# One selective-scan stage: C rows by broadcast transfers, two decay slots, seven drives on GpSimd, the sum three places behind

## The reference, cut to what matters

```python
sel = jnp.einsum('ble,se->bls', xc, sel_w)
dt_in = sel[..., :R_]
Bm = sel[..., R_:R_ + N_]
Cm = sel[..., R_ + N_:]
dt = jax.nn.softplus(jnp.einsum('blr,er->ble', dt_in, dt_w) + dt_b)
dA = jnp.exp(dt[..., None] * A)
dBu = dt[..., None] * Bm[:, :, None, :] * xc[..., None]
def step(h, inp):
    dA_t, dBu_t, C_t = inp
    h = dA_t * h + dBu_t
    y = jnp.einsum('ben,bn->be', h, C_t)
    return (h, y)
```

## Time and profile before

| | |
|---|---|
| time, median of 3 runs | 1578.91 us (1573.58 to 1582.68) |
| the profiled execution: its own time | 1573.16 us |
| its span in the trace | 1571.4 us |
| scan stage of one pair, first drive to last output instruction | about 129.5 us, four times |
| mean granted TensorE clock | 0.959 |

### The profile page before, as it was taken

How to read it: one execution, slowest core, us unless ns; L and a number is a source line. 1 busy time by engine, 2 the same in 40 slices (tenths; PEclk the granted TensorE clock), 3 DMA queues, 4 the chain that set the end, 5 groups by cost and what they waited for, 6 DMA issues and landing times. The chain is left out here.

```text
span 1571.4 us, 16757 instructions
## 1 busy us (share of the span) xinstructions
PE 1370.2 (87%) x5750; PEld 564.0 (36%) x5770; DVE 1079.3 (69%) x1253; ACT 689.0 (44%) x979; POOL 415.8 (26%) x242
## 2 busy tenths in 40 slices
PE   6877899988987779999997778999999777899897
PEld 2222233346422223325632222332563222333265
DVE  3598956674559995667455998556746699765673
ACT  0455543334245554324425554532541655543344
POOL 3256610012006660002100766000300276500040
PEclk9989999998999999999898999999989899999997
DMA  8100020000000002000000000200000000020000
GB/s 255 72 0 1 1 57 11 1 1 1 14 0 0 1 1 67 2 1 1 1 14 0 0 1 0 68 1 1 1 1 14 0 0 1 4 51 1 0 2 14
DMA packets 24692, 26.02 MB, mean 17 GB/s; under 512 B 4610, under 2 KB 21794, under 8 KB 24098
## 3 DMA queue, kind: packets, MB, share of 16 engines
q1 hardware_dynamic: 24002, 20.61, 4.5%
q10 hardware_dynamic: 608, 4.34, 0.9%
HBM read 20.73 MB, written 4.21 MB: 16 GB/s over the span
## 5 line engine op out<-in xcount | busy, mean ns | idle before, releaser
L405 POOL TENSOR_TENSOR scratch<-scratch 128x1024 f32<-128x1024 f32 x124 | 306.1, 2468 | 467.3 <-ACT scratch L872 312.1
L1081 DVE TENSOR_TENSOR_SCAN scratch<-ps,scratch 128x1024 f32<-128x1024 f32 x128 | 292.2, 2283 | 5.5 <-ACT ps L865 5.5
L551 PE MATMUL ps<-scratch,consts 128*128 128x512 f32 x512 | 255.6, 622 | 14.0 <-ACT work L896 12.0
L416 POOL TENSOR_TENSOR work<-work,rmax 128x512 f32<-128x512 f32 x64 | 67.4, 1053 | 614.3 <-DVE rmax L1231 614.3
L865 ACT ACTIVATE ps<-steps,vec 128x1024 f32<-128x1024 f32 x128 | 143.1, 1118 | 183.4 <-DVE scratch L1081 183.4
L1133 DVE TENSOR_TENSOR scratch<-scratch,ps 128x1024 f32<-128x1024 f32 x108 | 131.9, 1221 | 117.8 <-PE ps L610 114.8
L905 ACT ACTIVATE scratch<-ps 128x1024 f32<-128x1024 f32 x108 | 108.8, 1022 | 177.3 <-PE ps L597 177.3
L1073 DVE TENSOR_TENSOR scratch<-steps,ps 128x1024 f32<-128x1024 f32 x128 | 156.1, 1219 | 24.4 <-PE ps L525 16.3
L525 PE MATMUL ps<-bc,pick 128*128 128x512 bf16 x244 | 78.7, 402 | 98.6 <-DVE scratch L1073 97.5
L597 PE MATMUL ps<-h_odd,w 64*128 64x512 f32 x512 | 141.6, 639 | 3.8 <-ACT scratch L905 3.8
L610 PE MATMUL ps<-scratch,w 64*128 64x512 f32 x512 | 134.9, 602 | 8.1 <-DVE scratch L1133 8.1
(11 more groups left out here) (194 smaller groups left out, 1626.9 us busy)
## 6 DMA issues: line engine op xcount, KB each, us to landing
steps<-routed_table SPq DMA_DIRECT2D x128, 64.5 KB, 1.9
decayT<-in_decayT SPq DMA_DIRECT2D x8, 512.0 KB, 19.3
...
w<-in_w ACTq DMA_DIRECT2D x4, 512.0 KB, 19.5
out<-h_even SPq DMA_DIRECT2D x4, 512.0 KB, 2.6
bc<-in_x_next SPq DMA_DIRECT2D x3, 512.0 KB, 3.6
bc<-in_x_first SPq DMA_DIRECT2D x1, 512.0 KB, 4.5
```

The source lines that it names most:

```text
L405: pool.tensor_tensor(hc_slot(k), hs_slot(k), c_slot(k), ALU.mult).then_inc(sem["hc_ready"], 1)
L551: m = mm(ps[:, 6 + c, :], ident, hc_slot(k)[:, c * CH:(c + 1) * CH], start=(n == 0), stop=(n == NS - 1))
L1081: dve.tensor_tensor_scan(hs_slot(k), banks(DA_BANK), dbu_slot(k), 0.0, ALU.mult, ALU.add).then_inc(sem["scanned"], 1)
```

## The change

- C is no longer spread by PE and copied by ACT. The selected rows (16 B rows and 16 C rows) are copied from PSUM to SBUF as f32 (`c_rows`: DVE for the first sequence, ACT for the second), SP stores the 16 C rows to a DRAM tensor, and for each place SP loads one row of it onto all 128 partitions (`partition_broadcast`, 512 KB written), into one of three tiles. Load k waits for product k-3.
- The decay has two slots, banks 2-3 and 4-5; decay k waits for scan k-2.
- For seven places (5, 9, 13, 17, 21, 25, 29) the drive is made by POOL: PE spreads B for that place one position earlier (`B_ORDER`), ACT copies it to SBUF (`copy_b`, behind decay k-2), and POOL multiplies it by u in place, behind its product of place k-4. The other 25 drives stay on DVE.
- `sum_states` stands three places behind, and POOL's product has four tiles.
- The last place's product, in two halves, is made by DVE.

```diff
--- before.py
+++ after.py
...
+POOL_DRIVES = (5, 9, 13, 17, 21, 25, 29)
+B_ORDER = list(range(2 * NS))
+for _j in POOL_DRIVES:
+    B_ORDER[_j - 1:_j + 1] = [_j, _j - 1]
+C_RING = 3
...
-    b_ps=2 * NS, c_ps=2 * NS, dA_ready=2 * NS, c_sb=2 * NS, dbu_ready=2 * NS, scanned=2 * NS, hc_ready=2 * NS + 1,
+    b_ps=2 * NS, dA_ready=2 * NS, dbu_ready=2 * NS - len(POOL_DRIVES), b_copied=len(POOL_DRIVES),
+    dbu_pool=len(POOL_DRIVES), scanned=2 * NS, hc_ready=2 * NS - 1, hc_last=NC,
+    c_rows=2, c_stored=16 * 2, c_loaded0=16 * 11, c_loaded1=16 * 11, c_loaded2=16 * 10,
...
+        c_dram = nc.dram_tensor("c_rows", (2, NS, T), F32, kind="Internal").ap()
...
-        DA_BANK = 2
+        def dA_bank(k):
+            return 2 + 2 * (k % 2)
+        b_sb = work[:, 3 * T:4 * T]
+        def drives_up_to(k):
+            return k + 1 - sum(j <= k for j in POOL_DRIVES)
 
         def dbu_slot(k):
-            return scratch[:, 2 + k % 2]
+            return b_sb if k in POOL_DRIVES else scratch[:, 2 + drives_up_to(k) % 2]
 
         def c_slot(k):
-            return scratch[:, 4 + k % 2]
+            return scratch[:, (0, 1, 5)[k % C_RING]]
+        def c_landed(pair, k):
+            return sem[f"c_loaded{k % C_RING}"], at(pair, f"c_loaded{k % C_RING}", 16 * (k // C_RING + 1))
+        def c_rows(g):
+            return (work[0:32, 0:T] if g else work[0:32, 3 * T:4 * T])
...
-            return scratch[:, 9 + k % 3]
+            return scratch[:, (9, 10, 11, 4)[k % 4]]
...
+                sp.wait_ge(sem["c_rows"], at(pair, "c_rows", 1))
+                sp.dma_start(c_dram[0], c_rows(0)[NS:2 * NS]).then_inc(sem["c_stored"], 16)
+                sp.wait_ge(sem["c_stored"], at(pair, "c_stored", 16))
+                for k in range(2 * NS):
+                    g, n = divmod(k, NS)
+                    if k == C_RING:
+                        sp.wait_ge(sem["c_rows"], at(pair, "c_rows", 2))
+                        sp.dma_start(c_dram[1], c_rows(1)[NS:2 * NS]).then_inc(sem["c_stored"], 16)
+                    if k == NS:
+                        sp.wait_ge(sem["c_stored"], at(pair, "c_stored", 32))
+                    if k >= C_RING:
+                        sp.wait_ge(sem["hc_ready"], at(pair, "hc_ready", k - C_RING + 1))
+                    sp.dma_start(c_slot(k), c_dram[g, n].partition_broadcast(P))\
+                      .then_inc(sem[f"c_loaded{k % C_RING}"], 16)
...
-                for g in range(2):
-                    for n in range(NS):
-                        k = g * NS + n
-                        if k in U_LATE:
-                            c = U_LATE.index(k)
-                            cols = slice(c * NCH, (c + 1) * NCH)
-                            pool.wait_ge(sem["dt_late"], at(pair, "dt_late", c + 1))
-                            pool.tensor_tensor(u[:, 1, cols], dt[:, 1, cols], xc[:, 1, cols],
-                                               ALU.mult).then_inc(sem["u_late"], 1)
-                        pool.wait_ge(sem["scanned"], at(pair, "scanned", k + 1))
-                        pool.wait_ge(sem["c_sb"], at(pair, "c_sb", k + 1))
-                        if k >= 3:
-                            pool.wait_ge(sem["y_summed"], at(pair, "y_summed", k - 2))
-                        if k < 2 * NS - 1:
-                            pool.tensor_tensor(hc_slot(k), hs_slot(k), c_slot(k), ALU.mult).then_inc(sem["hc_ready"], 1)
-                for c in range(NC):
-                    cols = slice(c * CH, (c + 1) * CH)
-                    pool.tensor_tensor(hc_slot(k)[:, cols], hs_slot(k)[:, cols], c_slot(k)[:, cols],
-                                       ALU.mult).then_inc(sem["hc_ready"], 1)
+                for k in range(2 * NS - 1):
+                    if k in U_LATE:
+                        c = U_LATE.index(k)
+                        cols = slice(c * NCH, (c + 1) * NCH)
+                        pool.wait_ge(sem["dt_late"], at(pair, "dt_late", c + 1))
+                        pool.tensor_tensor(u[:, 1, cols], dt[:, 1, cols], xc[:, 1, cols],
+                                           ALU.mult).then_inc(sem["u_late"], 1)
+                    pool.wait_ge(sem["scanned"], at(pair, "scanned", k + 1))
+                    pool.wait_ge(*c_landed(pair, k))
+                    if k >= 4:
+                        pool.wait_ge(sem["y_summed"], at(pair, "y_summed", k - 3))
+                    pool.tensor_tensor(hc_slot(k), hs_slot(k), c_slot(k), ALU.mult).then_inc(sem["hc_ready"], 1)
+                    if k + 4 in POOL_DRIVES:
+                        j = k + 4
+                        pool.wait_ge(sem["u_ready"], at(pair, "u_ready", 1))
+                        if j >= NS:
+                            pool.wait_ge(sem["u_late"], at(pair, "u_late", NN))
+                        n_ = POOL_DRIVES.index(j) + 1
+                        pool.wait_ge(sem["b_copied"], at(pair, "b_copied", n_))
+                        pool.tensor_tensor(b_sb, u[:, j // NS, :], b_sb, ALU.mult).then_inc(sem["dbu_pool"], 1)
...
-                def spread_b(k):
+                def spread_b(i):
+                    k = B_ORDER[i]
...
-                    if k:
-                        pe.wait_ge(sem["dbu_ready"], at(pair, "dbu_ready", k))
+                    if i:
+                        last = B_ORDER[i - 1]
+                        if last in POOL_DRIVES:
+                            pe.wait_ge(sem["b_copied"], at(pair, "b_copied", POOL_DRIVES.index(last) + 1))
+                        else:
+                            pe.wait_ge(sem["dbu_ready"], at(pair, "dbu_ready", drives_up_to(last)))
...
-                def spread_c(k):
-                    g, n = divmod(k, NS)
-                    if k == 0:
-                        pe.wait_ge(sem["dt_read"], at(pair, "dt_read", 2))
-                    if k:
-                        pe.wait_ge(sem["c_sb"], at(pair, "c_sb", k))
-                    for c in range(NC):
-                        m = mm(ps[:, 4 + c, :], pick[:, NS + n:NS + n + 1].to_broadcast([P, P]),
-                               bc[:, g, c * CH:(c + 1) * CH], start=True, stop=True)
-                    m.then_inc(sem["c_ps"], 1)
                 def sum_states(k):
                     g, n = divmod(k, NS)
-                    pe.wait_ge(sem["hc_ready"], at(pair, "hc_ready", k + 1))
+                    if k < 2 * NS - 1:
+                        pe.wait_ge(sem["hc_ready"], at(pair, "hc_ready", k + 1))
                     if n == 0:
                         pe.wait_ge(sem["sel_read"], at(pair, "sel_read", 2))
+                        pe.wait_ge(sem["c_rows"], at(pair, "c_rows", 2))
...
-                            pe.wait_ge(sem["hc_ready"], at(pair, "hc_ready", 2 * NS + 1))
+                        if k == 2 * NS - 1:
+                            pe.wait_ge(sem["hc_last"], at(pair, "hc_last", c + 1))
...
-                LAG = 2
+                LAG = 3
...
-                    if k < 2 * NS:
-                        spread_c(k)
                     if k == 2 * NS:
 
-                        pe.wait_ge(sem["dbu_ready"], at(pair, "dbu_ready", 2 * NS))
+                        pe.wait_ge(sem["dbu_ready"], at(pair, "dbu_ready", PER["dbu_ready"]))
...
-                    if k:
-                        act.wait_ge(sem["scanned"], at(pair, "scanned", k))
+                    if k >= 2:
+                        act.wait_ge(sem["scanned"], at(pair, "scanned", k - 1))
+                    else:
+                        act.wait_ge(sem["dt_read"], at(pair, "dt_read", k + 1))
                     name = "dt_late" if k >= NS else "dt_ready"
                     act.wait_ge(sem[name], at(pair, name, PER[name]))
-                    act.activation(banks(DA_BANK), dt[:, k // NS, :], ACT.Exp, scale=v("A", k % NS))\
+                    act.activation(banks(dA_bank(k)), dt[:, k // NS, :], ACT.Exp, scale=v("A", k % NS))\
                        .then_inc(sem["dA_ready"], 1)
 
-                def copy_c(k):
-                    act.wait_ge(sem["c_ps"], at(pair, "c_ps", k + 1))
-                    if k >= 2:
-                        act.wait_ge(sem["hc_ready"], at(pair, "hc_ready", k - 1))
-                    act.activation(c_slot(k), banks(4), ACT.Copy).then_inc(sem["c_sb"], 1)
+                def copy_b(j):
+                    act.wait_ge(sem["b_ps"], at(pair, "b_ps", B_ORDER.index(j) + 1))
+                    n_ = POOL_DRIVES.index(j)
+                    if n_:
+                        act.wait_ge(sem["scanned"], at(pair, "scanned", POOL_DRIVES[n_ - 1] + 1))
+                    else:
+                        act.wait_ge(sem["c_stored"], at(pair, "c_stored", 16))
+                    act.activation(b_sb, banks(0), ACT.Copy).then_inc(sem["b_copied"], 1)
...
+                decay(0)
                 dt_above(1)
                 dt_size(1)
-                decay(0)
-                copy_c(0)
+                act.activation(c_rows(1), banks(SEL_BANK[1])[0:32], ACT.Copy).then_inc(sem["c_rows"], 1)
                 decay(1)
```

(26 more changed lines are left out.)

## The result

| | before | after |
|---|---|---|
| time, median of 20 runs each | 1575.81 us | 1570.66 us |
| the profiled execution: its own time; its span | 1573.16; 1571.4 us | 1570.53; 1568.7 us |
| scan stage, first scan to last output instruction, four pairs | 127.2 to 127.9 us | 126.7 to 126.8 us |
| mean granted TensorE clock | 0.959 | 0.937 |

The ratio after to before is 0.996 (95% interval 0.9949 to 0.9971). The change gives 5.2 us where 32 were forecast: 0.8 us a pair in the traces instead of 8.0. (One of the 20 executions before took 4255.88 us and stands outside the ratio.) The forecast started from a median of three runs, 1578.91 us; from 1575.81 the same 32 us would have led to 1544.

What follows compares the result with a forecast made beforehand. DVE was taken to bound the scan stage, busy 119.4 of 130 us in one pair. The terms summed to -8.0 us a pair, -32 for four pairs, from 1578.91 to 1547 us; the range was 1534 to 1585.

Steps and rivals of the forecast that it cites:

- the pace: Scan stage, steady part: four places take 13.39 us instead of 14.08, 4.8 us less per pair for seven groups.
- The chain "spread, copy, sum, spread": PE and ACT work before one drive in four: 2.93 us against 2.30 of cover, so that drive is 0.63 us late.
- The wait for the copy of the first sequence's sum: PE's idle before drive 19, which came 3.36 us late, was to go: -2.9 us a pair.
- the one before scan 31: DVE's wait for decay before scan 31, 1.19 us, was to go with the second decay slot: -1.2 us a pair.
- The stage's end: From scan 31's start to the first output instruction: 5.3 us against 4.85, +0.5 us a pair.
- rival 3: The broadcast load of C is slow: 1585 us at 8 us a load, 1628 at 9; chance 0.08.
- rivals 2 and 4: 2: GpSimd becomes the bound, 1574 us, chance 0.09. 4: drives gain nothing, chain 1.3 us late, 1566 us, chance 0.10.
- the port: SBUF access shared by DVE and GpSimd: no term in the sum; by the rule DVE's last product waits at most +0.2 us a pair.
- The credit of 1.9 us a pair: Small DVE instructions just ahead of drives 8, 12, 24 and 28 were to be swallowed by the 0.63 us stall.
- The term of +2.5 us a pair for the half clock: First group of the stage: its chain runs with PE at half clock, 5.4 us, 2.5 more than the others; bounds 0 and 5.
- Rival 1: PE's clock falls in the steady part, behind GpSimd's drive: 1607 us if once per group, 1577 every other group; chance 0.13.
- a clock below 0.9 in the steady part: Sign that the prediction is wrong: PE's clock in the scan stage's steady part was expected at 1.00.

Runs made afterwards that it cites:

- experiment 4: The changed kernel with the first sequence's output instructions on DVE (L1153, L1160) cut from 512 to 16 columns: 1567.83 us, one execution.
- Experiments 5 to 7: The changed kernel with matmuls on zeros keeping PE busy, 1571.68 us; with each small job as one full-width instruction, 1574.45 us; with both, 1558.29 us.
- experiments 10 and 11: The changed kernel with sums behind both spreads of a group, 1567.81 us; the same plus DVE's small jobs as single full-width instructions, 1548.82 us.

## Why the prediction was wrong, point by point

**What held.** The bound (DVE in the scan stage) and the pace: four places were to take 13.39 us and take 13.38 where no small instruction stands among them. The chain "spread, copy, sum, spread" was to make a drive 0.63 us late; it is 0.72 late. The wait for the copy of the first sequence's sum is gone, and so is the one before scan 31. The stage's end costs what was forecast: 1.79 us of waiting and 1.35 of half products against 2.56, so 0.58 for the +0.5. The load takes 3.7 us for the 3.6 taken from the nearest row, and is hidden (rival 3 is out). The time lies inside the range, nearer its slow end, next to rivals 2 and 4, but by neither of their mechanisms: GpSimd's product takes 2.45 us on average, as before (2.47), and the chain wasn't 1.3 us late. So the range held the time by luck.

**The step that failed: the port, which the sum put at nothing, with "+0.2 us a pair" beside it.** The working had row and rule in hand: a product of 2.86 us beside an all-SBUF DVE instruction, and the Trainium skill, page "SBUF — State Buffer", section "SBUF: two separate sides", by which such a DVE instruction and a GpSimd one exclude each other for a whole instruction. It asked only who else would be hurt on GpSimd's side, found drives and scans exempt (rightly: 1.22 and 2.28 us throughout), and applied it to the one product that moves. It didn't ask what the 32 small instructions on DVE, which all read two SBUF tiles, would meet once GpSimd is busy 94.95 us of 129 instead of 81.75 of 130 and starts its drive just as a scan ends. They were even credited with a gain. This term measured +5.0 us a pair, 20 in all. The trace of experiment 4 and that of the change agree with this rule of the Trainium skill both ways: 2.23 us for 16 columns, and +0.44 us for GpSimd where the DVE instruction comes first.

**The credit of 1.9 us a pair**, for small instructions swallowed by the 0.63 us stall, fell with it. Ahead of drives 8, 12, 24 and 28 the first pair has, between scan and drive, 0.40 us of small instruction and 0.96 of waiting, 2.46 and 0, 0.72 and 0.56, 2.76 and 0: 7.9 us where four times 0.63 were forecast. Two of these drives are preceded by the lock-outs in the fence above, both behind L447: GpSimd's drive starts as the copy ends, and that is as the scan ends.

**The term of +2.5 us a pair for the half clock was too small.** The place was right, the extent wasn't. The first group waits 3.07 us in the first pair and 2.54 to 2.59 in the others, and the second group waits again, 0.96 us in the first pair and 2.34 to 2.37 in the others, where the bound said "5 if second group has it too". The step that misled was "idles up to 2.4 us while GpSimd makes the drive": with place 5 not on DVE, PE has to sit out two scans and the small instructions between, 4.23 us. All waits of drives for PE come to 32.3 us, 7 over the terms of the sum.

**Rival 1**, the falling clock (the text before it calls it the second rival), came true in part. The prediction named a clock below 0.9 in the steady part as a sign of being wrong, and from 96 to 132 us it is 0.86, where the earlier trace rows had 1.00. The longest gaps are those that small instructions lengthen, but the clock also fell where none stands: behind the 2.74 us at 521.59, after which drive 16 is 1.04 late instead of 0.72. What such a fall costs there is small; the 2.5 us that the rival gave it came only in the first two groups, and then not in each pair in full. From 133 to 156 us of the first pair, where idles of 1.2 to 2.7 us alternate with bursts of work, the clock stays at 1.00; the same stretch of the other pairs (520.4 to 543.4 us, and so on) has 0.93. So the Trainium skill, page "TensorE: Matmul & The Clock Gate", section "A second HAM failure mode: psum-queue depth-cycling", by which short idles make the clock swing, is borne out in three pairs and not in the first.

**The frame of the sum.** Its terms were added as if independent. Experiments 5 to 7 show they aren't: a late DVE meets GpSimd less often, a punctual one more often, and a cure for either cost alone gives some 1 us a pair in the stage, both together 4. Nor is a gain in the stage kept to its full: what PE does behind it can be at another clock, 2.8 us a pair. A sum of waits at fixed lengths in one stage can't see either.

Open: what makes the clock fall behind one stage and not behind another, within one trace, and why an idle of 2.74 us is followed by either level. The falls behind the stages can move a time by some 9 us (the two groups of executions in experiments 10 and 11), so what a change in the stage is worth is read from the stage.
